# Second attention: the row maxima of the first half of a head in pairs of 64-row matmuls, with one VectorE reduction per pair

## The reference

```python
scores = jnp.einsum('bhid,bhjd->bhij', qr, kr) * scale
probs = jax.nn.softmax(scores, axis=-1)
out = jnp.einsum('bhij,bhjd->bhid', probs, v)
```

## Time and profile before

| | |
|---|---|
| time, median of 3 runs | 3351.94 us (3344.41 to 3352.87) |
| the profiled execution | 3346.46 us, its span 3344.7 us |
| second attention, both ends | about 2057 to 3170 us of the span |
| busy: TensorE, VectorE, ScalarE, GpSimd | 2978.6, 2775.2, 2989.8, 2504.1 us |

### The profile page before, as it was taken

How to read it: one execution, slowest core, us unless ns; L and a number is a source line. 1 busy time by engine, 2 the same in 40 slices (tenths; PEclk the granted TensorE clock), 3 DMA queues, 4 the chain that set the end, 5 groups by cost and what they waited for, 6 DMA issues and landing times. The chain is left out here.

```text
span 3344.7 us, 58506 instructions
## 1 busy us (share of the span) xinstructions
PE 2978.6 (89%) x19523; PEld 1261.6 (38%) x19523; DVE 2775.2 (83%) x4212; ACT 2989.8 (89%) x2783; POOL 2504.1 (75%) x1645
## 2 busy tenths in 40 slices
PE   6888888888888888888888796999999999999899
PEld 4222222212221222122211342566656665666548
DVE  7889999999999999999999896877777787778341
ACT  3999999999999999999999684799999999999832
POOL 5888888888888888888868363688688877887650
PEclk9797778877887788778877897999999999999999
DMA  2000000000000000000000264000110011001100
GB/s 71 12 8 8 5 2 7 7 7 0 7 7 7 0 7 7 7 0 7 7 10 1 68 214 115 27 27 27 43 35 27 27 27 51 27 27 27 35 9 14
DMA packets 59509, 85.23 MB, mean 25 GB/s; under 512 B 10064, under 2 KB 45904, under 8 KB 58960
## 3 DMA queue, kind: packets, MB, share of 16 engines
q1 hardware_dynamic: 59344, 82.93, 8.6%
HBM read 52.31 MB, written 30.54 MB: 25 GB/s over the span
## 5 line engine op out<-in xcount | busy, mean ns | idle before, releaser
L1266 POOL TENSOR_TENSOR lo<-pr,hi 128x1024 f16<-128x1024 f32 x384 | 813.0, 2154 | 217.1 <-ACT hi L1445 215.0
L1326 DVE TENSOR_REDUCE mx<-mx_ps 128x1 f32<-128x512 f32 x1024 | 664.1, 686 | 195.3 <-PE mx_ps L1488 190.7
L1461 ACT ACTIVATE pr<-s_ps 128x1024 f32<-128x1024 f32 x512 | 529.1, 1033 | 111.6 <-PE s_ps L1519 105.4
L1445 ACT ACTIVATE hi<-pr 128x1024 f16<-128x1024 f32 x512 | 545.3, 1065 | 0.0
L722 ACT ACTIVATE wt<-wt 128x2048 f32<-128x2048 f32 x256 | 485.2, 1896 | 0.5
L713 ACT ACTIVATE wt<-wt,theta_bias 128x2048 f32<-128x2048 f32 (+2 forms) x160 | 482.3, 3015 | 3.0 <-DVE wt L563 2.5
L501 POOL TENSOR_TENSOR wt<-base,wt 128x1024 f32<-128x1024 f32 x192 | 455.3, 2371 | 16.1
L501 POOL TENSOR_TENSOR wt<-vb,wt 128x1024 f32<-128x1024 f32 x192 | 454.9, 2369 | 16.0
L1538 PE MATMUL pv_ps<-vh,hi 128*128 128x129 f16 x4096 | 425.2, 220 | 11.3 <-POOL lo L1266 5.7
L1538 PE MATMUL pv_ps<-vh,lo 128*128 128x65 f16 x4096 | 411.2, 193 | 0.0
L1488 PE MATMUL mx_ps<-ka,qa 128*128 128x512 f16 x1024 | 360.0, 387 | 54.5 <-DMA ka<-qk 28.4
(11 more groups left out here) (210 smaller groups left out, 5021.7 us busy)
## 6 DMA issues: line engine op xcount, KB each, us to landing
qk<-stg SPq DMA_DIRECT2D x6, 2048.0 KB, 10.8
vh<-v SPq DMA_DIRECT2D x16, 520.0 KB, 3.4
qa<-qk SPq DMA_DIRECT2D x16, 512.0 KB, 3.5
ka<-qk SPq DMA_DIRECT2D x32, 256.0 KB, 4.9
v<-v_st SPq DMA_DIRECT2D x3, 2080.0 KB, 7.9
qst<-parts_dram SPq DMA_DIRECT2D x144, 32.0 KB
kst<-parts_dram SPq DMA_DIRECT2D x144, 32.0 KB
qk<-stg SPq DMA_DIRECT2D x4, 1024.0 KB, 7.9
```

The source lines that it names most:

```text
L1266: eng.tensor_tensor(lo[:, i % NHL, :, :], pr_slot(i), hi[:, i % NHL, :, :], ALU.subtract).then_inc(lo_done, 1)
L1326: eng.tensor_reduce(mx4[:, q // NCH, q % NCH:q % NCH + 1], mx_ps[:, q % 2, :], AX.X, ALU.max)\
L1445: eng.activation(hi[:, i % NHL, :, :], pr_slot(i), ACT.Copy).then_inc(hi_done, 1)
L1461: eng.activation(pr_slot(i), s_ps[:, i % 2, :, :], ACT.Exp, scale=SM).then_inc(exp_done, 1)
```

## The change

- The first 32 banks of heads 2 to 15 (those whose maxima are made in the steps of heads 1 to 14) go as 16 pairs: two matmuls of 64 rows each, one from rows 0 to 63 into the first PSUM bank, one from rows 64 to 127 into the second. They use only the high half of q. The second needs the high q in rows 64 to 127, so a fifth kind of load, `qc` (64 rows, 256 KB), goes out behind `qa`, into memory that is free in this stage (`two` in the rows of the order). `loaded` counts four transfers.
- VectorE reduces both banks of a pair in one instruction (128x1024 to 128x2).
- A new table sets where pairs and banks lie, by four places in a step: ahead of the scores, between their halves, behind them, and between the halves of `weigh`. By it steps 2 and 8 have two pairs, step 15 one pair and one bank, the other steps from 3 to 14 one pair; the last 32 banks lie in steps 15 to 26, 2 or 3 each.

```diff
+    NPAIR = 16
+    PAIR_US, BANK_US = 1.74, 0.69
+    SLOTS = 4
+    groups = [(2 * q, 2) for q in range(NPAIR)] + [(q, 1) for q in range(2 * NPAIR, NMX)]
+    span = PAIR_US * NPAIR + BANK_US * (NMX - 2 * NPAIR)
+    mx_slot = [SLOTS * MX0 + int(SLOTS * (MX1 - MX0) * (PAIR_US * min(n, NPAIR) + BANK_US * max(0, n - NPAIR)) / span)
+               for n in range(len(groups))]
...
+        qc = sb["xn2"].rearrange("p n d -> p (n d)").bitcast(F16).rearrange("p (a s) -> p a s", a=2)
...
                     for dst, src, sem_ in ((qa[:, par, :], q[h, :, :], loaded),
+                                           (qc[HD1:P, par, :], q[h, 0:HD1, :], loaded),
                                            (ka[0:HD1, par, :], k[h, 0:HD1, :], loaded),
...
-                def reduce_bank(h, q):
-                    eng.wait_ge(mx_done, NMX * h + q + 1)
-                    eng.tensor_reduce(mx4[:, q // NCH, q % NCH:q % NCH + 1], mx_ps[:, q % 2, :], AX.X, ALU.max)\
-                       .then_inc(mx_taken, 1)
+                def reduce_banks(h, q, n):
+                    eng.wait_ge(mx_done, NMX * h + q + n)
+                    j, c, b = q // NCH, q % NCH, q % 2
+                    eng.tensor_reduce(mx4[:, j, c:c + n], mx_ps[:, b:b + n, :], AX.X, ALU.max).then_inc(mx_taken, n)
...
                     if q == 0:
-                        eng.wait_ge(loaded, 16 * 3 * (h + 1))
+                        eng.wait_ge(loaded, 16 * 4 * (h + 1))
...
-                    eng.wait_ge(mx_taken, NMX * h + q + 1)
+                    eng.wait_ge(mx_taken, NMX * h + q + n)
...
+                        for b, (src, rows) in enumerate(((qa, slice(0, HD1)), (qc, slice(HD1, P)))):
+                            eng.matmul(mx_ps[:, b, :], src[rows, par, j * P:(j + 1) * P],
+                                       ka[rows, par, (c + b) * BANK:(c + b + 1) * BANK], start=True, stop=True)\
+                               .then_inc(mx_done, 1)
```

More of the change, by code:

```diff
@@ L1205, in stage_attention1, with maxima_in @@
     MX0, MX1 = 2, STEPS - 5
-    mx_at = [min(NMX, max(0, -(-NMX * (i - MX0) // (MX1 - MX0)))) for i in range(STEPS + 1)]
+    NPAIR = 16
[5 more added lines that the diff above has]
+               for n in range(len(groups))]
+    def maxima_in(i, slots=range(SLOTS)):
+        return [groups[n] for n in range(len(groups)) if mx_slot[n] // SLOTS == i and mx_slot[n] % SLOTS in slots]
     NQ1 = NMX // NS
@@ L1377, in one @@
                         if first:
-                            banks = [divmod(q, NMX) for q in range(first_at[i], first_at[i + 1])]
+                            banks = [(*divmod(q, NMX), 1) for q in range(first_at[i], first_at[i + 1])]
                         else:
-                            banks = [(h + 1, q) for q in range(mx_at[i], mx_at[i + 1])] if not last else []
+                            banks = [(h + 1, *group) for group in maxima_in(i)] if not last else []
                         cut = len(banks) // 2 if first else 1
@@ L1383, in one @@
                             first_row(i // 4)
-                        for hq, q in banks[:cut]:
-                            reduce_bank(hq, q)
+                        for at in banks[:cut]:
+                            reduce_banks(*at)
                         for n_ in (1, 0):
@@ L1389, in one @@
                                 low_half(h, at, n_)
-                        for hq, q in banks[cut:]:
-                            reduce_bank(hq, q)
+                        for at in banks[cut:]:
+                            reduce_banks(*at)
                         if first and i + 1 in TURN0:
@@ L1408, in _ @@
                 for q in range(NQ1):
-                    reduce_bank(0, q)
+                    reduce_banks(0, q, 1)
                 first_maxima(0)
@@ L1476, in _, with mx_banks @@
             def _(eng):
-                def mx_bank(h, par, q):
+                def mx_banks(h, par, q, n=1):
                     if q == 0:
-                        eng.wait_ge(loaded, 16 * 3 * (h + 1))
+                        eng.wait_ge(loaded, 16 * 4 * (h + 1))
                     if isinstance(h, int) and h == 0:
@@ L1485, in mx_bank @@
                         eng.wait_ge(mt_copied, h + NS)
-                    eng.wait_ge(mx_taken, NMX * h + q + 1)
+                    eng.wait_ge(mx_taken, NMX * h + q + n)
                     j, c = q // NCH, q % NCH
-                    eng.matmul(mx_ps[:, q % 2, :], qa[:, par, j * P:(j + 1) * P],
-                               ka[:, par, c * BANK:(c + 1) * BANK], start=True, stop=True).then_inc(mx_done, 1)
+                    if n == 1:
+                        eng.matmul(mx_ps[:, q % 2, :], qa[:, par, j * P:(j + 1) * P],
+                                   ka[:, par, c * BANK:(c + 1) * BANK], start=True, stop=True).then_inc(mx_done, 1)
+                    else:
+                        for b, (src, rows) in enumerate(((qa, slice(0, HD1)), (qc, slice(HD1, P)))):
+                            eng.matmul(mx_ps[:, b, :], src[rows, par, j * P:(j + 1) * P],
+                                       ka[rows, par, (c + b) * BANK:(c + b + 1) * BANK], start=True, stop=True)\
+                               .then_inc(mx_done, 1)
                 def mx_turn(h):
@@ L1502, in first_turn, with scores @@
                     eng.transpose(mx_ps[0:TS, 0, 0:P], mx[:, c * TS:(c + 1) * TS], ident[:, :]).then_inc(mt_ps, 1)
-                def scores(h, par, i):
+                def scores(h, par, i, between=()):
                     if isinstance(h, int) and h == 0:
@@ L1520, in scores, with weigh @@
                                         qb[0:HD1 + 1, par, w], start=False, stop=True)
-                    mm.then_inc(s_done, 1)
-                def weigh(h, par, i):
+                        if n_ == 1:
+                            mm.then_inc(s_done, 1)
+                        else:
+                            for at in between:
+                                mx_banks(*at)
+                def weigh(h, par, i, between=()):
                     c, kp = i // KP % NS, i % KP
@@ L1533, in weigh @@
                     for n_ in range(2):
+                        for at in between if n_ == 1 else ():
+                            mx_banks(*at)
                         k = 2 * kp + n_
@@ L1546, in one @@
                     for i in range(STEPS):
-                        q0, q1 = (mx_at[i], mx_at[i + 1]) if not (first or last) else (0, 0)
                         turns = first and i in TURN0
-                        fresh = [divmod(q, NMX) for q in range(first_at[i], first_at[i + 1])] if first else []
+                        early, inner, late, after = ([(h + 1, 1 - par, *group) for group in maxima_in(i, (slot,))]
+                                                     if not (first or last) else [] for slot in range(SLOTS))
+                        fresh = [(q // NMX, q // NMX, q % NMX) for q in range(first_at[i], first_at[i + 1])] if first else []
                         cut = 0 if turns else 2
[L1551 to L1554, removed]
+                        for at in early + fresh[:cut]:
+                            mx_banks(*at)
                         if i + 1 < STEPS:
-                            scores(h, par, i + 1)
+                            scores(h, par, i + 1, inner)
                         elif not last:
                             scores(h + 1, 1 - par, 0)
-                        for q in range(q0 + 1, q1):
-                            mx_bank(h + 1, 1 - par, q)
+                        for at in late:
+                            mx_banks(*at)
                         if turns:
@@ L1563, in one @@
                         else:
-                            for hq, q in fresh[cut:]:
-                                mx_bank(hq, hq, q)
+                            for at in fresh[cut:]:
+                                mx_banks(*at)
                         if i == MX1 + 1 and not last:
@@ L1568, in one @@
                         if i >= SUM or not first:
-                            weigh(h, par if i >= SUM else 1 - par, i - SUM)
+                            weigh(h, par if i >= SUM else 1 - par, i - SUM, after)
                         if turns:
-                            for hq, q in fresh:
-                                mx_bank(hq, hq, q)
+                            for at in fresh:
+                                mx_banks(*at)
                     if last:
@@ L1590, in _ @@
                 for q in range(NQ1):
-                    mx_bank(0, 0, q)
+                    mx_banks(0, 0, q)
                 first_turn(0)
```

## The result

| | |
|---|---|
| changed kernel, median of 4 runs | 3386.78 us (3378.66 to 3389.59) |
| kernel before, beside it | 3350.18 us (3344.41 to 3352.87) |
| ratio | 1.0107, 95% interval 1.0095 to 1.012 |

Slower by 36.6 us; the forecast was +23, range 3330 to 3405. The profiled execution took 3387.16 us, 40.7 above that of before.

The account below looks back on a forecast made before the run. TensorE was taken to set the pace while it makes maxima. Steps 5 to 26 (9), early heads (5.5), late heads (10.5), clock falls already paid (-2.9) and head 0 (1) gave +23 us: 3375 us, range 3330 to 3405.

Parts of the forecast that it names:

- Part 1: Head's load: qc ahead of ka lands the first pair 1.0 us later; the five late heads lose the clock.
- Part 2: TensorE: a pair's matmuls run at once in 0.22 us, plus 0.24 for the switch: 0.46 against 0.44 before.
- Free switch: Rival, faster: pairs run side by side and the array changes over at no cost; 3337 us, chance 0.22.
- Part 3: VectorE: reduction takes 1.22 us, starting 0.43 behind the matmul; pairs 1.70 apart, some 0.08 wait each at three places.
- Part 4: Steps 2 to 4: +5.5 us for nine early heads, +10.5 us for five late ones.
- the cliff: Step 2, early heads: low_half held behind GpSimd's second instruction, step 5 1.6 us later; if ahead, 0.4 sooner.
- the early ones mostly not: Wait for the load: the early heads, waiting 1.6 us, mostly keep the full clock.
- The +1 forecast for head 0: Head 0 waits for four transfers with nothing to cover them: +1 us.
- Part 5: Steps 5 to 26: 21.5 to 21.2 us in steps 5 to 14, 25.6 to 26.5 after; +0.65 a head.
- No delay: Rival, same: ka lands as before, the clock falls as before, low_half gets in ahead; 3355 us, chance 0.15.
- Pairs in series: Rival, slower: the two 64-row matmuls do not overlap, 49 us more; 3424 us, chance 0.13.

Follow-up runs that it names:

- b2: Changed kernel with qc of the next head loaded a head ahead, behind vh: 3358.54 us, ratio 1.0025.
- b3: Changed kernel with the last low half of step 2 ahead of the first reduction on VectorE: 3372.32 us, ratio 1.006.
- c1: Changed kernel with qc loaded a head ahead and step 2's last low half ahead of the first reduction: 3348.47 us, ratio 0.999.
- b4: Kernel before with the last low half of step 2 ahead of the first reduction on VectorE: 3333.2 us, ratio 0.9944.
- d2: Changed kernel with early qc, low half first, two reductions a pair, and maxima in steps 3 to 26: 3343.31 us, ratio 0.9987.
- c4: Kernel before with its banks in steps 3 to 26 in place of 2 to 26: 3331.62 us, ratio 0.9934.
- c3: As c1, but VectorE reduces a pair's two banks in two instructions of 512, not one of 1024: 3340.3 us, ratio 0.9975.
- c2: As c1, but each of a pair's matmuls has all 128 rows, and qc is not loaded: 3368.58 us, ratio 1.005.

## Why the prediction was right, and what was off

The time fell into the range and on the forecast's side, by the mechanism that it gave. Two agreements are luck: five heads lost the clock, as forecast, but they were two late and three early ones in place of five late ones; and an undisturbed head is as long as forecast by two errors that cancel. Point by point:

- *Part 1, the load*: right. The first pair stands at L of 7.0 to 7.9 in nine heads and 8.1 to 8.9 in five, forecast 7.3 and 8.4. Run b2 takes 28 us away by this load alone. The clock fell in two of the late heads, not in five: waits of 2.41, 2.78, and 3.04 us left it at 1.00, 2.89 and 3.24 did not.
- *Part 2, a pair on TensorE*: right in kind, 0.46 forecast and 0.41 measured. The switch is 0.19; it had been taken as 0.24 from a split by columns, whose way out is longer. The rival *Free switch* needed it below 0.14. Its sentence on the Trainium skill (TensorEngine Tiling (Array Packing), Key Properties) holds in kind: each change of mode costs time, 0.09 and 0.10 here, less than the full 0.16 each way.
- *Part 3, a pair on VectorE*: 1.225 was right, the start of 0.43 behind the pair was not: 0.52 to 0.53. The circle is 1.80 instead of 1.70, and the wait at a gap of three places some 0.2, not 0.08.
- *Part 4, steps 2 to 4*: the cliff was there, and about half of the early heads fell off it (five of nine). Made, step 5 begins at T+13.7 to 13.8, 0.6 to 0.7 sooner than the old T+14.4 (0.4 forecast); missed, with the clock kept, at T+15.76, 1.4 later (1.6 forecast); late with the clock kept the same 1.4, late with the clock lost 3.2 and 3.5 (2.1 forecast). **The step that failed is "the early ones mostly not"** lose the clock: I looked only at the wait for the load. In three early heads the clock fell at or just behind the second wait, 1.8 to 2.0 us for the reduction behind the held `low_half`; they are 1.3, 2.7 and 1.3 us above the 70.2 of a missed head. That the second wait did it is read from the order of time; run b3 shows that a first wait of 1.69 to 2.17 can do it alone. With the late heads at 15.9 us against 13.8 and the early ones at 18.7 against 11.4 this is the difference of 9.5 between the forecast's 22 and the 31.8 measured in the heads. The +1 forecast for head 0 came (20.88 us from its load to the next, 19.91 before).
- *Part 5, steps 5 to 26*: +0.65 forecast, +1.02 measured in the head of 2858.18 (from the first instruction of step 5 to the next load 54.47 us against 53.45). Steps 15 to 26 are about as forecast, +0.8 for +0.9. The term that was mis-sized is that of steps 5 to 14: 21.8 us where 21.2 was forecast and 21.6 had been. The waits at the gaps of three places, some 0.2 each and not 0.08, ate what was to be gained there. In the undisturbed head it does not show, since step 5 came 0.3 sooner than forecast: +0.31 in all, forecast +0.25. These are the two errors that cancel; c1 against b4, with 1.0 to 1.1 a head, and d2 against c4, with 0.85, bring the second to light.
- *The rivals*: *No delay* fell with the first row of L. *Pairs in series* fell with the two matmuls at the same 10 ns. What I had as no rival: that the old kernel stood behind a hold of its own, and that both repairs gain more than the change could.

Where the gain went: 224 VectorE instructions and their overhead are gone, but VectorE was not what TensorE waited for. It became that, since a pair takes both PSUM banks and nothing overlaps the reduction. The Trainium skill (TensorEngine Tiling (Array Packing), PSUM Bottleneck) says that tiling speeds up TensorE but not the emptying of PSUM; the circle of 1.80 us around a pair of 0.41 agrees.

What stays open: why waits of much the same length lose the clock in one head and not in another (1.62 in run c1 and 1.81 and 1.96 in the changed kernel with a fall, 1.95 and 3.04 there without). The Trainium skill (TensorE: Matmul & The Clock Gate, What's actually happening) says that the chip looks at activity at times of its own, not the kernel's. The mix of outcomes agrees, but no run here shows those times. Also open is what of the 8.9 us outside the heads belongs to the change; nearly 6 lie ahead of any changed line.

## What to carry to other kernels

An added transfer is paid where its consumer sits ahead of something with a deadline: here a first pair 0.1 to 0.4 us later made a head 2.0 us longer, or 3.3 to 4.6 with the clock lost. So look behind the wait for the next instruction that can be held, and for the wait that this makes. A unit of work that takes both halves of a double buffer takes the overlap away, whether one reduction empties them or two (run c3: the same 1.80); count the whole circle, from a matmul to the reduction's end and to the next matmul, against the spacing of the work.

## What the runs showed of the hardware

- Two 64-row matmuls in different halves of the array start 2 to 5 ns apart. Going in costs 0.09 us and coming out 0.10 (0.32 to the next instruction, of which 0.22 are the matmul).
- At the full clock, VectorE began 0.52 to 0.53 us after a pair when one instruction waited for both matmuls, 0.45 to 0.46 when two instructions waited one each, 0.43 after a single bank, and 0.70 after the first of two full matmuls (run c2). Why the first two differ by 0.06 was not tested.
- Two reductions of 512 in a row take 1.29 us (run c3), one of 1024 takes 1.23.
- A VectorE instruction with two SBUF inputs took 0.78 us when it began just ahead of a GpSimd instruction's end and 2.47 when it began just behind it.
